# Graph attention on one core: TensorE takes the score banks of a tile in pairs, and the value matmuls sorted by width

## Chip, cores, metric

The kernel runs on one NeuronCore of a Trainium2 chip (trn2). The metric is the device time of one execution in microseconds, lower is better.

## The reference

Inputs are x (2048 x 256), adj (2048 x 2048, about 0.4% of its entries not zero) and four weight matrices, all float32. Eight heads; head h takes the rows 256h to 256h+255 of the flat projections, since `reshape(h, n, d)` splits rows and not columns.

```python
q = (x @ Wq).reshape(h, n, d)          # Wq, Wk, Wv: 256 x 2048
k = (x @ Wk).reshape(h, n, d)
v = (x @ Wv).reshape(h, n, d)
a = jnp.einsum('hnd,hmd->hnm', q, k) * scale + adj + adj
mask = adj == 0.0
a = jax.nn.softmax(jnp.where(mask, -1000000.0, a), axis=-1)
a = jnp.where(mask, 0.0, a)
out = jnp.einsum('hnm,hmd->hnd', a, v)
out = out.transpose(1, 0, 2).reshape(n, h * d) @ Wout
return layernorm(x + out)
```

## The kernel before, in words

All matrix products run in float32r, each operand split into a high and a low part, and a product is made of high x high, high x low and low x high. Wout is folded into v, so that a head's values are already the output's 256 columns.

**Tiles.** The work is 8 heads x 16 tiles of 128 query rows, numbered tau = 16 h + t. A tile has 2048 key columns, in 4 banks of 512. `scores(tau, b)` (L398 to L412) makes one bank with six matmuls of 512 columns (L409). `values(tau, g)` (L414 to L435) multiplies the probabilities of four blocks of 128 keys with v: for each block one matmul of 512 columns (high part of p with both parts of v, L428 and L432) and one of 256 columns (low part of p with the high part of v, L430), into `y_bank`. The two are issued in turn, 256 then 512.

**Projections.** The projections of a head are made between the scores, from one 256 x 256 weight slice each: `k` (eight, c = 0 to 7), `q` (eight), `vt` (eight, x times Wv, turned) and `v` (eight, from vt and Wout). Each is twelve matmuls of 256 columns (L374). `x` is turned once per head (L394). The function `due(tau, b)` (L175 to L193) and the tables `FIRST_V`, `LATER_V`, `FIRST_K` and `NEXT_K` (L166 to L173) say which ones follow the scores of bank b in tile t. Within a head after the first: tile 0: k7, q1; tile 1: vt0; tile 2: vt1, q2, v0 to v3 and vt2 to vt5; tile 3: v4 to v7, vt6, vt7; tiles 4, 6, 8, 10, 12: one q; tile 13: the turn of the next x; tile 14: q0 of the next head; tile 15: k0 to k6 of the next head, as (k0), (k1, k2), (k3, k4), (k5, k6) behind the four banks. Tiles 5, 7, 9, 11 have none.

**Order on TensorE** (L441 to L453): for each tile, for each bank: six score matmuls, the projections due, then the values of bank g of tile tau - 3 (`LAG`). So a quiet tile is four times (6 of 512, then 4 times 256 + 512). The first value matmul of a tile waits until all four pieces of p are split (`p_lo`).

**Banks and evictions.** Scores and projections rotate through a ring of six PSUM banks, in the order in which they are issued; `own(key)` waits until the one six places before is emptied. A projection is evicted by ScalarE (`hi_of`, L526) and then VectorE (`lo_of`, L613 or L617); a score bank by VectorE (L630), which adds the mask and keeps the maximum. After the fourth bank VectorE takes the row maximum (L642), ScalarE exp (L532), VectorE the 32 x 32 transpose (L653), and DMAs on SP (L306) and on ScalarE's queue (L569) shuffle it in four pieces. ScalarE then copies each piece to the high part (`hi_p`, L541) and GpSimd subtracts for the low part (`lo_p`, L480). `hi_p` of tile tau - 2 runs in the round of tile tau; its first piece waits for `y_done`, the end of the values of two tiles earlier.

**Weights.** A slice is loaded by SP (L267) into one of five slots as soon as the projection five places earlier is done. ScalarE converts it (`hi_w`, L518) and GpSimd subtracts (`lo_w`, L469), and `project_x` waits for `w_lo` (L380). Both look ahead by the same count: after ScalarE has evicted the projection of weight n it converts up to weight n + 2 (L593 to L595), and GpSimd follows in the same place of its queue (L502 to L504):

```python
for b in range(BANKS):
    if 2 <= tau < ALL + 2 and b < 2:
        hi_p(tau - 2, 2 * b)
        hi_p(tau - 2, 2 * b + 1)
    ...
    for key in due(tau, b):
        hi_of(key)
        if key in w_order:
            hi_w(w_order[key] + 3)
```

So ScalarE's, GpSimd's, VectorE's and SP's queues all follow `due`: two pieces of p stand ahead of the projections of bank 0, the other two between those of bank 0 and of bank 1. SP loads the weights up to bank i's last key plus five before it shuffles piece i of the tile before (L331 to L335).

In head 0 the masks are built from adj by VectorE, ScalarE and GpSimd and stored; from head 1 on ScalarE's queue loads 1 MB per tile (`load_m`, L552).

Of the kernel before, what the change touches and what calls it, by code (L numbers as in the profile page):

```python
# [29 lines left out]
def graph_attention_layernorm(nc, x, adj, wq, wk, wv, wout, out):  # L30
# [14 lines left out]
    with ExitStack() as ctx:  # L45
# [113 lines left out]
        def in_order(key):  # L159
            give_home(key)  # L160
            if key[0] in ("k", "q", "vt"):
# [7 lines left out]
        LATER_V = {(1, 3): (("vt", 0),), (2, 0): (("vt", 1),), (2, 1): (("v", 0), ("vt", 2), ("v", 1), ("vt", 3)),  # L169
                   (2, 2): (("v", 2), ("vt", 4)), (2, 3): (("v", 3), ("vt", 5)), (3, 0): (("v", 4), ("vt", 6)),  # L170
                   (3, 1): (("v", 5), ("vt", 7)), (3, 2): (("v", 6), ("v", 7))}
# [4 lines left out]


# [69 lines left out]
        with nc.Block() as block:  # L247
# [111 lines left out]
            def _(pe):  # L359
# [6 lines left out]
                def wait_emptied(key):  # L366
                    r, fill = home[key]
                    pe.wait_ge(emptied[r], fill)
# [45 lines left out]
                def values(tau, g):  # L414
                    h, t = divmod(tau, TILES)
                    y = y_bank[tau % 2]
                    if g == 0:
                        pe.wait_ge(p_lo, 4 * (tau + 1))
                        if tau >= 2:
                            pe.wait_ge(y_added, tau - 1)  # L420
                    if t == 0:
                        wait_emptied(("v", h, 2 * g))
                        wait_emptied(("v", h, 2 * g + 1))
                    for j in range(TPB * g, TPB * (g + 1)):
                        hi, lo = (p_split[tau % 2][:, part, j * P:(j + 1) * P] for part in (HI, LO))
                        first, last = j == 0, j == CHUNKS - 1
                        if first:
                            nc.tensor.matmul(y[:], hi, v_split[:, j].rearrange("p s d -> p (s d)"),  # L428
                                             start=True, stop=False)
                        nc.tensor.matmul(y[:, 0:D], lo, v_split[:, j, HI], start=False, stop=False)  # L430
                        if not first:
                            mm = nc.tensor.matmul(y[:], hi, v_split[:, j].rearrange("p s d -> p (s d)"),  # L432
                                                  start=False, stop=last)
                    if g == BANKS - 1:
                        mm.then_inc(y_done, 1)  # L435
# [5 lines left out]
                for tau in range(ALL + LAG):  # L441
                    for g in range(BANKS):
# [9 lines left out]
                        if tau >= LAG:  # L452
                            values(tau - LAG, g)  # L453
# [352 lines left out]
```

## Time and profile before

| | |
|---|---|
| median of 3 runs | 1853.81 us (1853.4 to 1855.88) |
| the profiled execution | 1851.97 us, span 1850.2 us |
| TensorE matmul | 1808.3 us busy (98%), 10272 matmuls |
| TensorE weight loads | 1580.0 us (85%), beside the matmuls |
| VectorE, GpSimd, ScalarE | 1117.0, 983.8, 851.5 us |
| granted TensorE clock | 0.995 of full, mean over the span |
| chain of waits that ended last | 87% TensorE |

The span is cut by the profiler from the first to the last instruction; the run's own time is 1.8 us longer. Matmuls overlap: the next one starts before the last has drained, so what a matmul costs is the distance of starts, not the mean duration in the table of groups. A row of the timeline merges instructions of one line ("x6"), and the number in brackets at its end is the idle time of the engine before it with what ended it.

### The profile page before, as it was taken

What the parts mean: (1) busy time and instruction counts of PE and PEld (TensorE: products, weight loads), DVE (VectorE), ACT (ScalarE), POOL (GpSimd) and SP (SyncE); (2) the same over time, 40 slices, a digit from 0 to 9 for tenths busy, and PEclk for the clock granted to TensorE, in tenths of its full rate; (3) what the DMA queues carried; (4) which work ended last, traced back from release to release, by engine and by line L of the source; (5) the groups of instructions that cost most, each with busy time, mean ns of one, the idle gap of its engine ahead of it and who ended that gap; (6) DMA issues with size and microseconds to landing.
All of it is one profiled execution on the core that took longest, in us unless ns stands there. A gap on an engine that the chain in (4) does not pass through costs nothing.

```text
span 1850.2 us, 29363 instructions
## 1 busy us (share of the span) xinstructions
PE 1808.3 (98%) x10272; PEld 1580.0 (85%) x10272; DVE 1117.0 (60%) x2316; ACT 851.5 (46%) x1411; POOL 983.8 (53%) x764
## 2 busy tenths in 40 slices
PE   7989899999999999999999999999999999999997
PEld 6978788888898888988889888888888888898886
DVE  6788855555555555555655555555555556556667
ACT  4645554344554444544454444544454444554442
POOL 6787765444644446444564445634455444544443
PEclk9999999999999999999999999999999999999999
DMA  7787765666656666566664666656665566655664
GB/s 229 226 283 238 249 211 156 177 191 186 195 147 187 191 195 182 150 185 186 199 187 143 194 185 190 181 157 194 189 187 168 160 197 196 189 166 155 180 180 116
DMA packets 186962, 345.96 MB, mean 187 GB/s; under 512 B 39360, under 2 KB 96704, under 8 KB 170432
## 3 DMA queue, kind: packets, MB, share of 16 engines
q1 hardware_dynamic: 146112, 193.06, 37.2%
q10 hardware_dynamic: 40704, 151.03, 25.5%
q8 instruction: 82, 1.34, 0.3%
q14 instruction: 64, 0.52, 0.1%
HBM read 190.84 MB, written 18.87 MB: 113 GB/s over the span
## 4 chain that ended last, share of the span: by engine, by line
PE 87%; DVE 3%; issue 1%; SPq 1%; DMA 0%; POOL 0%; ACT 0%; DVEq 0%; ACTq 0%
PE bank L409 34%; PE y_bank L432 22%; PE bank L374 17%; PE y_bank L430 12%; PE y_bank L428 1%; SPq L306 1%; DVE blocks L653 1%; DVE zero_mark L691 0%; DVE y_acc L743 0%; POOL p_split L480 0%; DVE t_p L630 0%; DVE m_sb L697 0%; DMA raw_x<-in_x_dram 0%; PE bank L394 0%; ACT m_sb L560 0%
## 5 line engine op out<-in xcount | busy, mean ns | idle before, releaser
L480 POOL TENSOR_TENSOR p_split<-p_turned,p_split 128x512 fp32r<-128x512 f32 x512 | 651.5, 1301 | 628.7 <-ACT p_split L541 628.1
L409 PE MATMUL bank<-k_split,q_split 128*128 128x512 f32 x3072 | 790.0, 392 | 0.0
L432 PE MATMUL y_bank<-v_split,p_split 128*128 128x512 f32 x1920 | 701.8, 399 | 0.0
L409 PEld LDWEIGHTS bank<-k_split,q_split 128*128 128x128 f32 x3072 | 577.4, 188 | 110.5 <-issue 0.3
L630 DVE CUSTOM_DVE_ANT_0 t_p<-bank,m_sb 128x512 f32<-128x512 f32 x512 | 351.2, 687 | 339.9 <-PE bank L409 317.5
L430 PE MATMUL y_bank<-v_split,p_split 128*128 128x256 f32 x2048 | 555.7, 282 | 0.0
L532 ACT ACTIVATE t_p<-t_p,small 128x2048 f32<-128x2048 f32 x128 | 256.8, 2006 | 442.3 <-DVE small L642 442.3
L432 PEld LDWEIGHTS y_bank<-v_split,p_split 128*128 128x128 f32 x1920 | 362.7, 189 | 76.1
L430 PEld LDWEIGHTS y_bank<-v_split,p_split 128*128 128x128 f32 x2048 | 389.1, 190 | 18.7
L541 ACT ACTIVATE p_split<-p_turned 128x512 fp32r<-128x512 f32 x512 | 291.9, 620 | 167.1 <-DMA p_turned<-blocks 166.9
L653 DVE STREAM_TRANSPOSE blocks<-t_p 128x2048 f32<-128x2048 f32 x128 | 295.9, 2312 | 106.3 <-ACT t_p L532 74.1
L469 POOL TENSOR_TENSOR w_slot<-raw_w,w_slot 128x512 fp32r<-128x512 f32 x192 | 250.1, 1305 | 199.5 <-ACT w_slot L518 197.4
L374 PE MATMUL bank<-x_t,w_slot 128*128 128x256 f32 x2304 | 305.2, 284 | 11.6 <-issue 9.7
L374 PEld LDWEIGHTS bank<-x_t,w_slot 128*128 128x128 f32 x2304 | 296.5, 192 | 23.0 <-issue 11.9
L518 ACT ACTIVATE w_slot<-raw_w 128x512 fp32r<-128x512 f32 x192 | 119.7, 623 | 12.6 <-DMA raw_w<-in_L_gnn_Wk_dram 9.8
L374 PEld LDWEIGHTS bank<-w_out,vt_split 128*128 128x128 f32 x768 | 98.7, 191 | 6.1 <-POOL w_out L474 2.8
L374 PE MATMUL bank<-w_out,vt_split 128*128 128x256 f32 x768 | 101.2, 283 | 2.4 <-POOL w_out L474 2.4
L675 DVE SCALAR_TENSOR_TENSOR y_acc<-y_bank,small,y_acc 128x256 f32<-128x256 f32 x128 | 61.9, 484 | 48.8 <-PE y_bank L432 48.5
L486 POOL TENSOR_TENSOR m_sb<-m_sb,blocks 128x512 f32<-128x512 f32 x46 | 76.8, 1682 | 21.0 <-ACT m_sb L560 20.5
L526 ACT ACTIVATE v_split<-bank 128x512 fp32r<-128x512 f32 x64 | 38.2, 596 | 91.1 <-PE bank L374 91.1
L526 ACT ACTIVATE vt_split<-bank 128x512 fp32r<-128x512 f32 x64 | 38.3, 598 | 88.6 <-PE bank L374 88.6
L613 DVE SCALAR_TENSOR_TENSOR q_split<-bank,q_split 128x512 fp32r<-128x512 f32 x64 | 44.2, 690 | 52.9 <-ACT q_split L526 52.9
(45 smaller groups left out, 716.3 us busy)
## 6 DMA issues: line engine op xcount, KB each, us to landing
m_sb<-m_dram ACTq DMA_DIRECT2D x112, 1024.0 KB, 5.4
p_turned<-blocks SPq DMA_DIRECT2D x1536, 64.0 KB, 2.2
p_turned<-blocks ACTq DMA_DIRECT2D x512, 64.0 KB, 2.3
raw_w<-in_L_gnn_Wk_dram SPq DMA_DIRECT2D x64, 256.0 KB, 3.8
blocks<-in_adj_dram SPq DMA_DIRECT2D x64, 256.0 KB, 4.4
raw_w<-in_L_gnn_Wq_dram SPq DMA_DIRECT2D x64, 256.0 KB, 3.7
m_dram<-m_sb SPq DMA_DIRECT2D x16, 1024.0 KB, 6.6
raw_w<-in_L_gnn_Wv_dram SPq DMA_DIRECT2D x64, 256.0 KB, 3.8
```

Source lines behind the costliest of these rows:

```text
L374: mm = nc.tensor.matmul(dst[:, o * R:(o + 1) * R], left[:, a, k, o * P:(o + 1) * P], right[:, b, k, :], start=(i == 0), stop=(i == len(TER ...
L409: mm = nc.tensor.matmul(dst[:], q[:, a, k, f * P:(f + 1) * P], k_split[:, kk, k, b * BANK:(b + 1) * BANK], start=(i == 0), stop=(i == len( ...
L430: nc.tensor.matmul(y[:, 0:D], lo, v_split[:, j, HI], start=False, stop=False)
L432: mm = nc.tensor.matmul(y[:], hi, v_split[:, j].rearrange("p s d -> p (s d)"), start=False, stop=last)
L469: nc.gpsimd.tensor_tensor(w[:, LO], raw_slot[n % SLOTS][:], w[:, HI].bitcast(F32), ALU.subtract).then_inc(w_lo, 1)
L480: nc.gpsimd.tensor_tensor(lo, p_turned[:, i * BANK:(i + 1) * BANK].rearrange("p (j b) -> p j b", b=QUAD), hi.bitcast(F32), ALU.subtract).t ...
L486: nc.gpsimd.tensor_tensor(m_piece(a), m_piece(a), adj_place[q].rearrange("p (r c) -> p c r", c=C), ALU.add).then_inc(m_by_pool, 1)
L518: nc.scalar.activation(w[:, HI], raw_slot[n % SLOTS][:], ACT.Copy).then_inc(w_hi, 1)
L532: nc.scalar.activation(t_p[:], t_p[:], ACT.Exp, bias=neg_max[:, t:t + 1], scale=1.0, accum_out=row_sum[:, t:t + 1]).then_inc(exp_done, 1)
L541: nc.scalar.activation(by_chunk(p_split[tau % 2][:, HI])[:, :, i, :], p_turned[:, i * BANK:(i + 1) * BANK].rearrange("p (j b) -> p j b", b ...
L630: nc.vector.tensor_tensor_reduce(out=t_p[:, b * BANK:(b + 1) * BANK], in0=bank[r][:], in1=m_sb[tau % 2][:, b * BANK:(b + 1) * BANK], scale ...
L653: nc.vector.transpose(turned_place(tau)[:].rearrange("p (q j b) -> p j q b", q=QUADS, b=QUAD), t_p[:].rearrange("p (j q b) -> p j q b", q= ...
```

## The change

TensorE takes two banks at a time: twelve score matmuls, the projections due in both banks, then the values of two banks, first eight matmuls of 512 columns and then eight of 256. `due` yields nothing at even banks and the keys of both banks at odd ones, on every engine. In a head after the first, v0 to v3 and v4 to v7 are moved so that a part of v is overwritten only after the values of the head before have read it: tile 2 makes v0 vt2 v1 vt3 v2 vt4 v3 vt5 behind bank 3, tile 3 makes v4 vt6 v5 vt7 v6 v7 behind bank 1. Tile 15 makes k0 k1 k2 behind bank 1 and k3 k4 k5 k6 behind bank 3. The number of matmuls and their operands are unchanged, and so are all waits, but for their place.

```diff
--- before.py
+++ after.py
@@ -166,14 +166,20 @@
         FIRST_V = {(0, 3): (("vt", 0), ("vt", 1)), (1, 0): (("v", 0), ("vt", 2)), (1, 1): (("v", 1), ("vt", 3)),
                    (1, 2): (("v", 2), ("vt", 4)), (1, 3): (("v", 3), ("vt", 5)), (2, 0): (("v", 4), ("vt", 6)),
                    (2, 1): (("v", 5), ("vt", 7)), (2, 2): (("v", 6),), (2, 3): (("v", 7),)}
-        LATER_V = {(1, 3): (("vt", 0),), (2, 0): (("vt", 1),), (2, 1): (("v", 0), ("vt", 2), ("v", 1), ("vt", 3)),
-                   (2, 2): (("v", 2), ("vt", 4)), (2, 3): (("v", 3), ("vt", 5)), (3, 0): (("v", 4), ("vt", 6)),
-                   (3, 1): (("v", 5), ("vt", 7)), (3, 2): (("v", 6), ("v", 7))}
+        LATER_V = {(1, 3): (("vt", 0),), (2, 0): (("vt", 1),), (2, 2): (("v", 0), ("vt", 2), ("v", 1), ("vt", 3)),
+                   (2, 3): (("v", 2), ("vt", 4), ("v", 3), ("vt", 5)), (3, 0): (("v", 4), ("vt", 6)),
+                   (3, 1): (("v", 5), ("vt", 7), ("v", 6), ("v", 7))}
         FIRST_K = {(0, 0): (4, 5), (0, 1): (6, 7)}
         NEXT_K = {(TILES - 1, 0): (0,), (TILES - 1, 1): (1, 2), (TILES - 1, 2): (3, 4), (TILES - 1, 3): (5, 6)}
 
         def due(tau, b):
 
+
+            if b % 2:
+                yield from due_by_bank(tau, b - 1)
+                yield from due_by_bank(tau, b)
+
+        def due_by_bank(tau, b):
 
             h, t = divmod(tau, TILES)
             if h >= H:
@@ -411,27 +417,24 @@
                                               start=(i == 0), stop=(i == len(TERMS) - 1))
                     mm.then_inc(scores_done, 1)
 
-                def values(tau, g):
+                def values(tau, pair):
                     h, t = divmod(tau, TILES)
                     y = y_bank[tau % 2]
-                    if g == 0:
+                    if pair == 0:
                         pe.wait_ge(p_lo, 4 * (tau + 1))
                         if tau >= 2:
                             pe.wait_ge(y_added, tau - 1)
                     if t == 0:
-                        wait_emptied(("v", h, 2 * g))
-                        wait_emptied(("v", h, 2 * g + 1))
-                    for j in range(TPB * g, TPB * (g + 1)):
-                        hi, lo = (p_split[tau % 2][:, part, j * P:(j + 1) * P] for part in (HI, LO))
-                        first, last = j == 0, j == CHUNKS - 1
-                        if first:
-                            nc.tensor.matmul(y[:], hi, v_split[:, j].rearrange("p s d -> p (s d)"),
-                                             start=True, stop=False)
-                        nc.tensor.matmul(y[:, 0:D], lo, v_split[:, j, HI], start=False, stop=False)
-                        if not first:
-                            mm = nc.tensor.matmul(y[:], hi, v_split[:, j].rearrange("p s d -> p (s d)"),
-                                                  start=False, stop=last)
-                    if g == BANKS - 1:
+                        for c in range(4 * pair, 4 * (pair + 1)):
+                            wait_emptied(("v", h, c))
+                    chunks = range(2 * TPB * pair, 2 * TPB * (pair + 1))
+                    for j in chunks:
+                        nc.tensor.matmul(y[:], p_split[tau % 2][:, HI, j * P:(j + 1) * P],
+                                         v_split[:, j].rearrange("p s d -> p (s d)"), start=(j == 0), stop=False)
+                    for j in chunks:
+                        mm = nc.tensor.matmul(y[:, 0:D], p_split[tau % 2][:, LO, j * P:(j + 1) * P],
+                                              v_split[:, j, HI], start=False, stop=(j == CHUNKS - 1))
+                    if pair == BANKS // 2 - 1:
                         mm.then_inc(y_done, 1)
 
                 pe.wait_ge(ident_ready, 1)
@@ -449,8 +452,8 @@
                                 project_v(key)
                             else:
                                 project_x(key)
-                        if tau >= LAG:
-                            values(tau - LAG, g)
+                        if tau >= LAG and g % 2:
+                            values(tau - LAG, g // 2)
 
             @block.gpsimd
             def _(pool):
```

## Rows read from the trace of the kernel before

**Rows 1.** The page, part 1: busy us (share of the span) xinstructions of each engine.

```profile
PE 1808.3 (98%) x10272; PEld 1580.0 (85%) x10272; DVE 1117.0 (60%) x2316; ACT 851.5 (46%) x1411; POOL 983.8 (53%) x764
```

**Rows 2.** Windows: stretch and length in us, busy (x), PEclk, DMA share, GB/s.

```profile
400.00:1800.00 1400.00, 1400.00 (x7979) 1.00 0.61 180
...
795.09:806.22 11.13, 11.13 (x58) 9.40 (x57) 6.43 (x14) 4.37 (x8) 5.07 (x4) 1.00 0.63 182
```

**Rows 3.** Timeline of TensorE in a tile without projections: start us, us, instruction.

```profile
797.88 1.52 PE L409 MATMUL bank<-k_split,q_split 128*128 128x512 f32 x6
799.24 0.28 PE L430 MATMUL y_bank<-v_split,p_split 128*128 128x256 f32 x1
...
800.64 1.54 PE L409 MATMUL bank<-k_split,q_split 128*128 128x512 f32 x6
802.02 0.28 PE L430 MATMUL y_bank<-v_split,p_split 128*128 128x256 f32 x1
```

**Rows 4.** Timeline of TensorE early in head 0, runs of one width.

```profile
44.23 1.55 PE L409 MATMUL bank<-k_split,q_split 128*128 128x512 f32 x6
45.62 1.60 PE L374 MATMUL bank<-w_out,vt_split 128*128 128x256 f32 x12
47.05 1.60 PE L374 MATMUL bank<-x_t,w_slot 128*128 128x256 f32 x12
48.49 1.55 PE L409 MATMUL bank<-k_split,q_split 128*128 128x512 f32 x6
```

**Rows 5.** Timeline of TensorE, tile 15 of head 3 and the next start.

```profile
913.99 1.54 PE L409 MATMUL bank<-k_split,q_split 128*128 128x512 f32 x6
...
919.59 3.04 PE L374 MATMUL bank<-x_t,w_slot 128*128 128x256 f32 x24
...
925.26 3.04 PE L374 MATMUL bank<-x_t,w_slot 128*128 128x256 f32 x24
928.13 0.28 PE L430 MATMUL y_bank<-v_split,p_split 128*128 128x256 f32 x1
...
935.21 0.62 PE L409 MATMUL bank<-k_split,q_split 128*128 128x512 f32 x2
```

**Rows 6.** Timeline of ScalarE and its DMA queue in the same tile.

```profile
913.82 0.33 ACTq L552 DMA_DIRECT2D m_sb<-m_dram  x1
...
916.00 1.14 ACT L541 ACTIVATE p_split<-p_turned 128x512 fp32r<-128x512 f32 x2
...
919.49 0.63 ACT L541 ACTIVATE p_split<-p_turned 128x512 fp32r<-128x512 f32 x1 [0.83 <-DMA p_turned<-blocks]
921.22 0.60 ACT L526 ACTIVATE k_split<-bank 128x512 fp32r<-128x512 f32 x1 [1.10 <-PE bank L374]
...
926.89 0.60 ACT L526 ACTIVATE k_split<-bank 128x512 fp32r<-128x512 f32 x1 [3.11 <-PE bank L374]
```

**Rows 7.** Timeline of GpSimd in the same tile.

```profile
919.21 1.31 POOL L469 TENSOR_TENSOR w_slot<-raw_w,w_slot 128x512 fp32r<-128x512 f32 x1
920.49 2.55 POOL L480 TENSOR_TENSOR p_split<-p_turned,p_split 128x512 fp32r<-128x512 f32 x2
...
928.09 2.72 POOL L469 TENSOR_TENSOR w_slot<-raw_w,w_slot 128x512 fp32r<-128x512 f32 x2 [2.54 <-ACT w_slot L518]
```

**Rows 8.** TensorE waits on weights, heads 0 and 1; windows at two waits of head 0.

```profile
243.90 1.72 PE L374 MATMUL bank<-x_t,w_slot 128*128 128x256 f32 x12 [3.65 <-issue]
...
299.31 1.67 PE L374 MATMUL bank<-x_t,w_slot 128*128 128x256 f32 x12 [1.18 <-issue]
...
187.00:192.00 5.00, 2.36 (x12) 1.00 0.94 335
...
245.00:250.00 5.00, 5.00 (x22) 0.66 0.36 111
```

**Rows 9.** Timeline of VectorE: the eviction behind ScalarE's at 921.22.

```profile
921.85 0.69 DVE L617 TENSOR_TENSOR k_split<-bank,k_split 128x512 fp32r<-128x512 f32 x1 [1.10 <-ACT k_split L526]
```

**Rows 10.** Timeline of ScalarE: the last exp.

```profile
1821.42 2.01 ACT L532 ACTIVATE t_p<-t_p,small 128x2048 f32<-128x2048 f32 x1 [6.76 <-DVE small L642]
```

## Prediction

> **What bounds the kernel now.** I read the engine totals first: TensorE is busy 1808.3 us of a span of 1850.2, and nothing else passes 1117 [rows 1]. The windows then say where the missing 42 us lie. From 400 to 1800 us TensorE is busy in all 1400 us at a granted clock of 1.00 [rows 2]; its idle time is outside: the start, the building of the masks in head 0, the first head switch, and the end. So from head 1 on the time is the length of TensorE's own queue: an edit pays only if it makes that queue shorter, and any new wait in it is paid in full.
>
> The queue's length has to be read from starts, since durations overlap. In the timeline of a quiet tile six score matmuls take 1.36 us from the first's start to the next group's (0.2267 each), the four pairs of value matmuls that follow 1.40, and six score matmuls right behind such pairs 1.38 [rows 3]. Where runs of one width follow each other, twelve 256-column matmuls take 1.43 to 1.44 (0.1196 each) and six 512-column ones behind them 1.38 to 1.39 [rows 4]. In alternation a 256 and a 512 cost 0.350; apart they cost 0.2267 + 0.1196 = 0.346, and every bank's scores pay for the return as well. Coming back from 256 to 512 costs some 0.026 once, over the next six matmuls.
>
> **Part 1, the value matmuls in runs.** A tile without projections takes 11.13 us [rows 2]. After: 40 of 512 x 0.2267 = 9.07, two returns x 0.026 = 0.05, 16 of 256 x 0.119 = 1.91 (the first of a run follows in 0.114), together 11.03: 0.10 less. A tile with projections keeps those runs as they are, but has one return more: 0.07 to 0.09 less. By the tables five tiles of a later head have none; the head gains 5 x 0.10 + 11 x 0.08 = 1.39 us. Seven heads: -9.7. Head 0 waits for data in half of its tiles; I take -0.5 of a possible -1.3. Term: **-10.2**.
>
> Eight 512-column value matmuls in a row don't occur in the trace. If alternation is not what costs, the term is 0; if the 256-column ones also ran at half the clean 512 (0.1133), it would be 2048 x 0.006 = 12 us more. I stay at the row of the same width. What speaks against the change is a rule of the Trainium skill, "TensorE: Matmul & The Clock Gate", Back-to-back issue gap: spacing is columns over 2.4 GHz plus 2.5 ns, whatever the neighbour, 215.8 and 109.2 ns. By it the order is worth nothing and the sum would be 10.2 higher. The rows give 226.7 and 119.6, and more in alternation, so here the rows disagree with it.
>
> **Part 2, bank 3's scores come earlier in the tile.** They now end 2.8 us before the tile's end, not 1.4, so maximum, exp and transpose start 1.4 earlier. In mid-kernel TensorE waits for none of them: 0. At the end it counts: the last exp starts at 1821.42 [rows 10], the split of tile 126 follows, and values(126) waits for it, values(127) behind it. That chain moves up 1.4: **-1.4**. In head 0 scores of bank 1 now stand ahead of the wait for p_lo, which shortens single waits by up to 1.4; but the x turn in tile 13 waits for its load and now has one more value group behind it. Together 0, bounds -5 and +4.
>
> **Part 3, projections of two banks stand in a row.** This is the dear part. A weight is prepared only two keys ahead: ScalarE converts w(n+2) after it has evicted projection n (L518 behind L526), GpSimd subtracts (L469), and TensorE waits for w_lo. From ScalarE's eviction start to GpSimd's end is 926.89 to 928.09 + 1.3 = 2.5 us [rows 6, 7]; with the step from the last matmul to ScalarE (the first projection begun at 919.59 ends its 1.44 at 921.03, ScalarE starts at 921.22: 0.19) 2.7 us. Today four value pairs and six scores (2.8) stand between two groups and cover it. In a row there is one projection between n and n+2: 1.44 [rows 4]. Two places of each head switch have three or more weights of one kind in a row.
>
> (a) Tile 15, second pair: k3 k4 k5 k6 stand in a row. Today k5 starts two blocks after k4 ends at 928.13; its weight is ready at 929.4 [rows 5, 7]. After: k5 waits 1.3, and the restart behind a wait costs 0.07 (twelve matmuls take 1.67 instead of 1.60 [rows 4, 8]). k6's weight is then ready in time. 1.35 x 7 = **+9.5**.
>
> (b) Tile 15, first pair: k0 k1 k2. TensorE reaches k2 at start + 2.77 + 2.88 = 5.65 us. Its weight is converted after k0's eviction, and in ScalarE's and GpSimd's queues all four pieces of the p split of tile 13 now stand ahead of it; today only two do (GpSimd runs L469 between two pairs of L480). GpSimd's four pieces take 2 x 2.55 = 5.1 [rows 7]. They start 0.7 after ScalarE's first, which waits for exp and y_done: today start + 2.0 (916.00 against 913.99 [rows 5, 6]), after the change some + 0.7. GpSimd: 1.4 + 5.1 + 1.3 = 7.8, so at least 2.2 of wait. But the fourth piece also waits for its shuffle, which lands behind the 1 MB mask load issued at 913.82: ScalarE takes it at 919.49, 5.7 after that issue [rows 6]. The mask load moves up 2.5, together with q's weight load and the shuffle itself. Landing at + 5 to + 6 gives k2's weight at 8.3 to 9.5 and a wait of 2.6 to 3.9. I take 3.0 for six heads: **+18**. Head 0's switch already waits 3.65 there today [rows 8]; two more pieces of 1.27 stand ahead: **+2.5**.
>
> (c) Tile 3: v7 follows vt7 with only v6 between, and needs vt7 evicted by ScalarE and VectorE: 0.19 + 0.63 + 0.69 [rows 6, 9] plus a wake-up is 1.6 against 1.44. 0.25 x 7 = **+1.8**. Tile 2's eight projections alternate v and vt, so weights stand 2.9 apart and vt two projections ahead of its v: 0.
>
> That two keys are too few is to be seen today: in tile 2 of head 1, where five projections stand in one bank and the p pieces came late, the fifth waited 1.18 us [rows 8].
>
> **Queues passed.** SP loads weights before it shuffles a piece. With all keys on odd banks pieces 0 and 2 no longer wait for projections, and 1 and 3 wait for the pair's last, which TensorE reaches a value group earlier than today: 0 for TensorE, as p_lo has time to spare (tile 13's is complete at 923.0 and its use begins after 935.2 [rows 5, 7]). ScalarE's own shuffles are no longer behind bank 2's eviction: earlier. The ring of six banks: after the eight projections each bank was filled 7 us before, evictions keep up; k7's eviction, now behind the p pieces, has 3 us left before bank 3 of the new head needs it. If that cover went, it would be 1 us per head.
>
> **Sum.** -10.2 - 1.4 + 9.5 + 18 + 2.5 + 1.8 = +20.2. The profiled execution took 1851.97 us (span 1850.2 and 1.8 around it): 1872.2. The median of the three runs shown is 1.8 higher than the profiled run, which would give 1874; I keep to the profiled one, as the runs' own spread is 2.5, and about 0.2% (3.7 us) is what can be told from no change. Forecast **1872**.
>
> **Rivals.**
> 1. *The clock falls too.* At head 0's switch TensorE was idle 3.65 us and the next window shows a clock of 0.66; at 187 to 192, with 2.36 of 5 us busy and so 2.64 idle, it stayed at 1.00 [rows 8]. A wait of 3.0 to 3.9 lies between. A window of 5 us at 0.66 costs 1.7; at six switches +10: 1882.
> 2. *The weights come in time* (faster than before): ScalarE or GpSimd runs further ahead than I schedule, so terms a to c are 0 and only -11.6 stays: 1840. It turns at a total wait of 1.7 us per switch: below that the change gains. For it: both engines are idle about half the time [rows 1]. Against: k2's and k5's conversions are behind an eviction in a fixed queue, and two waits of this kind are in the trace.
> 3. *The order of widths is free* (the rule above). Nothing is gained in the values, the waits stay: 1852 + 31.8 - 1.4 = 1882. Against: the alternation's extra is there in the rows [rows 3, 4] and in every quiet tile.
> 4. *The waits are at their lower ends* (k2 2.2, k5 1.2, v7 0, head 0 +0.5, and head 0 gains 3): 13.2 + 8.4 + 0.5 - 11.6 - 3 = +7.5: 1859.5.
>
> **Chances.** Forecast 0.52 (1864 to 1879), rival 1 0.17, rival 2 0.13, rival 3 0.04, rival 4 0.11, and 0.03 for waits of such a size that they cancel the gain. Faster 0.13, same 0.03, slower 0.84. The range reaches from rival 4's lower side to above rival 1: 1852 to 1888; it leaves out rival 2. Within the likeliest case it is 1864 to 1879.
>
> **What would show it.** Tiles without projections at 11.03 instead of 11.13 (part 1). New rows "PE L374 <- POOL w_slot L469" or "<- issue", two per head near the start and the second half of tile 15, of about 3.0 and 1.3 (a, b); a small L374 wait on VectorE's vt_split in tile 3 (c). TensorE's busy time in mid-kernel below 100%. The last exp 1.4 nearer to the end of the scores. If the L374 waits are missing, or add to less than 12 us, the forecast is wrong; if the granted clock shows 0.5 stretches at each switch, rival 1 holds.

## The result and the profile after

The changed kernel takes 1889.87 us (median of 6 runs, 1886.65 to 1895.1) where the kernel before takes 1856.34 in the same series: ratio 1.0183, 95% interval 1.0167 to 1.0199, some 34 us slower. The profiled executions are 1890.11 and 1851.97 us, 38.1 apart. Forecast were 1872 and a range up to 1888: the direction is right, the size is not.

The page of the changed kernel, its first part (against [rows 1]; its span is 1888.3 us):

```profile
PE 1817.1 (96%) x10272; PEld 1596.7 (85%) x10272; DVE 1160.5 (61%) x2316; ACT 853.1 (45%) x1411; POOL 983.3 (52%) x764
```

TensorE has 9 us more of busy time for the same 10272 matmuls, and idles 29 us more. Its waits between 400 and 1830 us (us in total, times, longest); before there was none on a weight there:

```profile
PE bank L380 <- issue: 21.0, 12, 3.4
```

These are twelve waits at the six switches from head 1 to head 7. The starts of the tiles in both timelines of TensorE tell where the 38.1 us lie: up to the start of head 1 +14.2 (273.89 against 259.68), in head 1 +2.7, in heads 2 to 6 +23.5, in head 7 and the end -2.4.

**A quiet tile**, head 3 tile 5 (against [rows 2, 3]; L415 scores, L432 the 512-column value matmuls, L435 the 256-column ones, start and us first):

```profile
815.96 2.91 PE L415 MATMUL bank<-k_split,q_split 128*128 128x512 f32 x12
818.70 1.98 PE L432 MATMUL y_bank<-v_split,p_split 128*128 128x512 f32 x8
820.52 1.11 PE L435 MATMUL y_bank<-v_split,p_split 128*128 128x256 f32 x8
...
826.98 1.32 PE L415 MATMUL bank<-k_split,q_split 128*128 128x512 f32 x5
```

From 815.96 to 826.98 are 11.02 us; before it was 11.13 [rows 2]. Twelve scores and eight values of 512 columns take 4.56 together (0.228 each with the return), eight of 256 take 0.95 (0.119 each), as the runs of one width did before [rows 4].

**Tile 15 of head 3** (against [rows 5]; L380 are the projections), up to the start of head 4:

```profile
934.00 2.91 PE L415 MATMUL bank<-k_split,q_split 128*128 128x512 f32 x12
936.74 3.03 PE L380 MATMUL bank<-x_t,w_slot 128*128 128x256 f32 x24
941.83 2.20 PE L380 MATMUL bank<-x_t,w_slot 128*128 128x256 f32 x12 [2.06 <-issue]
943.83 3.07 PE L432 MATMUL y_bank<-v_split,p_split 128*128 128x512 f32 x8
...
947.68 2.91 PE L415 MATMUL bank<-k_split,q_split 128*128 128x512 f32 x12
950.42 3.03 PE L380 MATMUL bank<-x_t,w_slot 128*128 128x256 f32 x24
954.62 3.13 PE L380 MATMUL bank<-x_t,w_slot 128*128 128x256 f32 x24 [1.16 <-issue]
...
960.38 0.86 PE L415 MATMUL bank<-k_split,q_split 128*128 128x512 f32 x3
```

26.4 us instead of 21.2. k0 and k1 are the 24 matmuls at 936.74; k2 starts only at 941.83. In the second pair k5 starts at 954.62, behind 1.16 us of idleness. And one thing more: the eight value matmuls at 943.83 take 3.07 us where the same eight take 2.00 at 957.58 and 1.98 in the quiet tile. They are slow, not late.

The timeline of GpSimd in that tile (against [rows 7]; L483 pieces of p, L472 weights):

```profile
935.29 5.21 POOL L483 TENSOR_TENSOR p_split<-p_turned,p_split 128x512 fp32r<-128x512 f32 x4 [1.40 <-ACT p_split L544]
940.46 2.50 POOL L472 TENSOR_TENSOR w_slot<-raw_w,w_slot 128x512 fp32r<-128x512 f32 x2
...
953.25 1.27 POOL L472 TENSOR_TENSOR w_slot<-raw_w,w_slot 128x512 fp32r<-128x512 f32 x1 [6.71 <-ACT w_slot L521]
```

The timeline of ScalarE and its DMA queue (against [rows 6]; L555 mask load, L544 pieces of p, L529 eviction, L521 weight):

```profile
931.42 0.39 ACTq L555 DMA_DIRECT2D m_sb<-m_dram  x1
...
934.59 1.67 ACT L544 ACTIVATE p_split<-p_turned 128x512 fp32r<-128x512 f32 x3
938.51 0.63 ACT L544 ACTIVATE p_split<-p_turned 128x512 fp32r<-128x512 f32 x1 [2.26 <-DMA p_turned<-blocks]
939.05 0.58 ACT L529 ACTIVATE k_split<-bank 128x512 fp32r<-128x512 f32 x1
939.53 0.62 ACT L521 ACTIVATE w_slot<-raw_w 128x512 fp32r<-128x512 f32 x1
```

GpSimd subtracts four pieces of p (5.21 us from 935.29) before it comes to k2's weight at 940.46; TensorE could have used that weight at 939.6. The shuffle of the fourth piece, which I had feared behind the mask load of 931.42, came only just in time: ScalarE took that piece at 938.51 and ended its copy at 939.14, GpSimd was through with the third at 939.11 and began the fourth at 939.23. Heads 1, 2, 3, 4 and 6 are alike in this, within 0.4 us. In head 5 the shuffle was late, and the wait for k2 is the longest of the six. ScalarE's fourth piece there, and TensorE's k2:

```profile
1397.52 0.63 ACT L544 ACTIVATE p_split<-p_turned 128x512 fp32r<-128x512 f32 x1 [3.59 <-DMA p_turned<-blocks]
```

```profile
1400.82 2.90 PE L380 MATMUL bank<-x_t,w_slot 128*128 128x256 f32 x12 [3.37 <-issue]
```

For k5 the weight's turn on GpSimd comes at 953.25, behind the eviction of k3.

**The clock.** Windows of TensorE in this tile (stretch, length, busy, PEclk, DMA share, GB/s):

```profile
935.00:940.00 5.00, 4.78 (x33) 1.00 0.53 169
940.00:945.00 5.00, 3.17 (x15) 0.77 0.40 115
945.00:950.00 5.00, 5.00 (x25) 0.89 0.70 186
```

and at the switches of head 1 and head 5:

```profile
480.00:485.00 5.00, 3.82 (x29) 1.00 0.49 146
485.00:490.00 5.00, 4.02 (x26) 1.00 0.54 157
1398.00:1403.00 5.00, 2.18 (x10) 0.71 0.36 113
```

At the ends of heads 2 to 6 the granted clock fell to its lower level (1.2 of 2.4 GHz) about where the wait for k2 ends, in head 5 for twice as long. In head 1 it stayed at 1.00, though the wait for k2 was 2.15 us there and 2.01 to 2.28 in heads 2, 3, 4 and 6. Tile 15 took 24.93 us in head 1, and 26.33, 26.38, 26.61, 28.91 and 26.52 in heads 2 to 6. With the idle time of its two waits taken off, that is 1.54 to 1.56 us more than in head 1 for heads 2, 3, 4 and 6, and 2.76 for head 5.

**Head 0.** Waits of TensorE there, the longest among them:

```profile
20.15 2.10 PE L415 MATMUL bank<-k_split,q_split 128*128 128x512 f32 x6 [2.44 <-DVE k_split L620]
...
72.71 2.90 PE L380 MATMUL bank<-x_t,w_slot 128*128 128x256 f32 x12 [3.83 <-issue]
...
209.85 1.66 PE L415 MATMUL bank<-k_split,q_split 128*128 128x512 f32 x6 [1.91 <-DVE small L633]
218.61 1.09 PE L400 MATMUL bank<-ident,raw_x 128*128 128x128 f32 x4 [7.11 <-DMA raw_x<-in_x_dram]
...
254.27 2.90 PE L380 MATMUL bank<-x_t,w_slot 128*128 128x256 f32 x12 [5.57 <-issue]
```

20.15: scores of bank 1 now follow bank 0's at once and need k3 evicted. 72.71: tile 2 makes v4 vt6 q2 v5 vt7 in a row, three weights of one stretch. 209.85 waits for VectorE to empty a bank, 218.61 for the load of the next x: 7.1 us, where it was 4.3. 254.27 is k2 at head 0's switch.

### The profile page after: what moved, and what is told of

It is laid out like the page before. It is cut to its first block, busy times and chain, and to the rows that moved or that the text cites. A ratio compares the mean times of both kernels' runs of the same rounds, so it can differ in the third digit from the quotient of the medians.

```text
span 1888.3 us, 29363 instructions
## 1 busy us (share of the span) xinstructions
PE 1817.1 (96%) x10272; PEld 1596.7 (85%) x10272; DVE 1160.5 (61%) x2316; ACT 853.1 (45%) x1411; POOL 983.3 (52%) x764
## 3 DMA queue, kind: packets, MB, share of 16 engines
q8 instruction: 82, 1.34, 0.3%
## 4 chain that ended last, share of the span: by engine, by line
PE 85%; SPq 3%; DVE 2%; issue 2%; DMA 1%; POOL 0%; ACT 0%; ACTq 0%; DVEq 0%
PE bank L415 33%; PE y_bank L432 22%; PE bank L380 17%; PE y_bank L435 11%; SPq L312 2%; DMA p_turned<-blocks 1%; DVE blocks L656 1%; DVE y_acc L746 0%; POOL p_split L483 0%; DVE zero_mark L694 0%; DMA raw_x<-in_x_dram 0%; PE bank L400 0%; DVE t_p L633 0%; ACTq L572 0%; ACT m_sb L563 0%
## 5 line engine op out<-in xcount | busy, mean ns | idle before, releaser
L483 POOL TENSOR_TENSOR p_split<-p_turned,p_split 128x512 fp32r<-128x512 f32 x512 | 651.0, 1298 | 618.8 <-ACT p_split L544 617.4
L415 PE MATMUL bank<-k_split,q_split 128*128 128x512 f32 x3072 | 746.9, 392 | 6.5 <-DVE k_split L620 4.0
L415 PEld LDWEIGHTS bank<-k_split,q_split 128*128 128x128 f32 x3072 | 560.5, 189 | 114.0 <-issue 5.3
L432 PE MATMUL y_bank<-v_split,p_split 128*128 128x512 f32 x2048 | 519.3, 396 | 4.0 <-POOL p_split L483 4.0
L432 PEld LDWEIGHTS y_bank<-v_split,p_split 128*128 128x128 f32 x2048 | 384.8, 192 | 80.9 <-POOL p_split L483 4.8
L544 ACT ACTIVATE p_split<-p_turned 128x512 fp32r<-128x512 f32 x512 | 292.6, 621 | 253.4 <-DMA p_turned<-blocks 253.2
L472 POOL TENSOR_TENSOR w_slot<-raw_w,w_slot 128x512 fp32r<-128x512 f32 x192 | 247.9, 1296 | 246.8 <-ACT w_slot L521 246.5
L380 PE MATMUL bank<-x_t,w_slot 128*128 128x256 f32 x2304 | 312.3, 290 | 41.4 <-issue 35.3
L380 PEld LDWEIGHTS bank<-x_t,w_slot 128*128 128x128 f32 x2304 | 301.6, 197 | 52.6 <-issue 43.9
L435 PEld LDWEIGHTS y_bank<-v_split,p_split 128*128 128x128 f32 x2048 | 279.6, 190 | 20.3
L435 PE MATMUL y_bank<-v_split,p_split 128*128 128x256 f32 x2048 | 285.6, 282 | 0.0
L521 ACT ACTIVATE w_slot<-raw_w 128x512 fp32r<-128x512 f32 x192 | 119.7, 624 | 12.2 <-DMA raw_w<-in_L_gnn_Wk_dram 10.7
L380 PE MATMUL bank<-w_out,vt_split 128*128 128x256 f32 x768 | 103.6, 285 | 2.2 <-POOL w_out L477 2.0
L663 DVE SCALAR_TENSOR_TENSOR small<-small 128x1 f32<-128x1 f32 x128 | 103.3, 807 | 0.0
L380 PEld LDWEIGHTS bank<-w_out,vt_split 128*128 128x128 f32 x768 | 98.2, 193 | 5.1 <-POOL w_out L477 2.4
L620 DVE TENSOR_TENSOR k_split<-bank,k_split 128x512 fp32r<-128x512 f32 x64 | 44.0, 690 | 64.6 <-ACT k_split L529 64.4
L529 ACT ACTIVATE k_split<-bank 128x512 fp32r<-128x512 f32 x64 | 37.9, 592 | 89.9 <-PE bank L380 89.8
```

The source lines that it names most:

```text
L380: mm = nc.tensor.matmul(dst[:, o * R:(o + 1) * R], left[:, a, k, o * P:(o + 1) * P], right[:, b, k, :], start=(i == 0), stop=(i == len(TER ...
L415: mm = nc.tensor.matmul(dst[:], q[:, a, k, f * P:(f + 1) * P], k_split[:, kk, k, b * BANK:(b + 1) * BANK], start=(i == 0), stop=(i == len( ...
L432: nc.tensor.matmul(y[:], p_split[tau % 2][:, HI, j * P:(j + 1) * P], v_split[:, j].rearrange("p s d -> p (s d)"), start=(j == 0), stop=False)
L435: mm = nc.tensor.matmul(y[:, 0:D], p_split[tau % 2][:, LO, j * P:(j + 1) * P], v_split[:, j, HI], start=False, stop=(j == CHUNKS - 1))
L472: nc.gpsimd.tensor_tensor(w[:, LO], raw_slot[n % SLOTS][:], w[:, HI].bitcast(F32), ALU.subtract).then_inc(w_lo, 1)
L483: nc.gpsimd.tensor_tensor(lo, p_turned[:, i * BANK:(i + 1) * BANK].rearrange("p (j b) -> p j b", b=QUAD), hi.bitcast(F32), ALU.subtract).t ...
```

## The experiments

The theory after this reading (W): the weights' look-ahead of two keys covers the distance of banks, not projections in a row; its waits carry most of the loss, and the clock falls because of them. Beside it (H): in head 0 the projections in a row meet the building of the masks. Rivals: the waits come from the pieces of p or the loads, pairing as such costs, the sorting costs, or the clock falls without the waits.

**1. Look-ahead three** (label look3).

```diff
-                                lo_w(w_order[key] + 3)
+                                lo_w(w_order[key] + 4)
-                                hi_w(w_order[key] + 3)
+                                hi_w(w_order[key] + 4)
```

> The changed kernel with one edit: ScalarE and GpSimd prepare weights three keys ahead instead of two. Theory W (the waits on weights in tile 15 carry the loss, and the clock falls because of them): both waits of each switch go (k2's weight is then made behind q0 of the tile before, k5's behind k2), 7 x (2.3 + 1.4) = 26 us, and with them the half-clock stretches of heads 1 to 6, about 9 us; 1852 to 1858 in all, tile 15 of heads 1 to 6 at 21.1 us. What stays above the kernel before is head 0. Rival S (the waits come from the p pieces or the shuffles standing ahead in ScalarE's queue, whatever the look-ahead): k2's wait stays, 1875 or more. Rival C (the clock falls from the longer runs of 256-column matmuls, not from the waits): waits go but the granted clock still shows one 0.5 stretch per switch, about 1863.

Measured: 0.9987 (0.9978 to 0.9997), median 1851.41. The timeline of TensorE, starts of tile 15 of head 3 and of head 4:

```profile
921.81 2.91 PE L415 MATMUL bank<-k_split,q_split 128*128 128x512 f32 x12
...
942.95 1.32 PE L415 MATMUL bank<-k_split,q_split 128*128 128x512 f32 x5
```

Tile 15 takes 21.14 us in all of heads 1 to 6, no wait of TensorE is left from 300 to 1830 us, and no half-clock stretch between 262 and 1839. The two characters edited give back 36 us. Theory W holds; rivals S and C fall. Head 1 starts at 271.8 us, so most of head 0's loss stays, and the heads behind it take 223.5 us instead of 224.6.

**2. Only the sorting** (sort_only), on the kernel before:

```diff
-                    for j in range(TPB * g, TPB * (g + 1)):
...
+                    chunks = range(TPB * g, TPB * (g + 1))
+                    for j in chunks:
+                        nc.tensor.matmul(y[:], p_split[tau % 2][:, HI, j * P:(j + 1) * P],
+                                         v_split[:, j].rearrange("p s d -> p (s d)"), start=(j == 0), stop=False)
+                    for j in chunks:
+                        mm = nc.tensor.matmul(y[:, 0:D], p_split[tau % 2][:, LO, j * P:(j + 1) * P],
+                                              v_split[:, j, HI], start=False, stop=(j == CHUNKS - 1))
```

> The kernel before with one part of the change: the eight value matmuls of a bank as four of 512 and then four of 256 columns; banks one by one, projections where they were. Theory W: a bank is 10 x 0.2267 + 0.026 + 0.47 = 2.77 us instead of 2.79, a quiet tile 11.06 to 11.07 instead of 11.13, 128 tiles: 7 to 8 us less, 1844 to 1846, no new wait. Rival (the order of widths is free): 11.13 and 1852. Rival (sorting itself brings the loss, as p_lo or v are needed in another order): above 1856 with waits at L428.

Measured: 0.9979 (0.9969 to 0.9988), median 1850.02. A quiet tile, from the start of its scores to the next tile's:

```profile
793.82 1.55 PE L409 MATMUL bank<-k_split,q_split 128*128 128x512 f32 x6
...
804.89 1.32 PE L409 MATMUL bank<-k_split,q_split 128*128 128x512 f32 x5
```

11.07 us, as worked out. The gain in time (4 us by the ratio, and between the profiled executions) is less than the 7 to 8 expected, which took 0.06 for all 128 tiles: a quiet tile gains that, the others in heads 2 to 6 mostly 0.03 to 0.05, so a head takes 223.95 us for 224.59. Head 0 is 0.9 shorter up to head 1's start, and head 1 takes 0.5 longer.

**3. Projections with their own bank** (keys_by_bank), else as changed:

```diff
-            if b % 2:
-                yield from due_by_bank(tau, b - 1)
-                yield from due_by_bank(tau, b)
+            yield from due_by_bank(tau, b)
```

> The changed kernel with one part undone: the projections stay with their own bank on every engine (scores 0, its projections, scores 1, its projections, then the values of both banks); the value matmuls and the tables for v as in the change. Theory W: k0 and k1, and k4 and k5, have six score matmuls (1.38) between them, which with one projection makes 2.8 us against the 2.7 that a weight needs; at most 0.1 to 0.3 of wait per place, quiet tiles at 11.03; head 0 near the kernel before: 1841 to 1847, clock at 1.00 after head 0. Rival (pairing the banks on TensorE is what costs, not where the projections stand): 1870 or more.

Measured: 0.9971 (0.9960 to 0.9982), median 1848.65. Tile 15 of head 3 and head 4's start:

```profile
914.66 1.55 PE L413 MATMUL bank<-k_split,q_split 128*128 128x512 f32 x6
...
935.93 1.32 PE L413 MATMUL bank<-k_split,q_split 128*128 128x512 f32 x5
```

21.27 us: 0.12 above look-ahead three, with two more returns from 256 to 512 columns in it, so six score matmuls between k0 and k1 all but cover the weight. Pairing on TensorE is not what costs; where the projections stand is. Head 1 starts at 264.1 us, 4.4 later than before, which is why the time lies above the 1841 to 1847 expected.

**4. Head 0 in the old order** (head0_old): `due` by bank and values by bank for tau < 16.

```diff
-            if b % 2:
+            if tau < TILES:
+                yield from due_by_bank(tau, b)
+            elif b % 2:
...
-                        if tau >= LAG and g % 2:
+                        if LAG <= tau < TILES:
+                            values_by_bank(tau - LAG, g)
+                        elif tau >= LAG and g % 2:
```

> The changed kernel, with head 0 (its 16 tiles) in the order of the kernel before on all engines and heads 1 to 7 as changed. Theory W plus H (head 0 loses 14 us by itself, as its projections in a row meet the building of the masks on VectorE and the late load of the next x): first tile of head 1 starts near 260 us instead of 273.9, the rest as in the change, 1876 in all. Rival (head 0's loss is made up later, or is a consequence of the same weight waits): no better than 1885.

Measured: 1.0141 (1.0124 to 1.0158), median 1879.25; head 1 starts at 262.0 us. The waits of heads 1 to 6 are nearly the same, 12 times, 21.0 us. Head 0 is worth 8 us by the ratios and 12 by the starts of head 1. The clock fell at the switches of heads 2 to 5; at those of heads 1 and 6 it stayed at 1.00 behind waits of 2.12 and 2.21 us, and tile 15 took 24.89 and 24.99 us.

**5. k2 moved behind bank 3** (k2_moved), look-ahead two:

```diff
-        NEXT_K = {(TILES - 1, 0): (0,), (TILES - 1, 1): (1, 2), (TILES - 1, 2): (3, 4), (TILES - 1, 3): (5, 6)}
+        NEXT_K = {(TILES - 1, 0): (0,), (TILES - 1, 1): (1,), (TILES - 1, 2): (2, 3, 4), (TILES - 1, 3): (5, 6)}
```

> The changed kernel (look-ahead two) with one key moved: tile 15 makes k0 k1 behind bank 1 and k2 k3 k4 k5 k6 behind bank 3, so the first of the two waits has no place and five keys stand in a row. Theory W: no wait in the first half of tile 15; in the row, k4's weight is made behind k2's eviction and waits 1.3, k6's is then nearly in time: 1.4 to 1.6 in all, tile 15 at 22.5 to 22.8 us in heads 1 to 6 instead of 24.9 to 28.9. Theory K (the clock falls because of the 2.2 us wait): no half-clock stretch in heads 1 to 6, 1862 to 1868 in all. Rival (the fall comes from the sum of the waits of a tile or from any wait over 1 us): a stretch per head remains, tile 15 at 24.2 or more, 1873.

Measured: 1.0086 (1.0072 to 1.0099), median 1871.14. Tile 15 of head 3 in the timeline of TensorE:

```profile
924.37 2.91 PE L415 MATMUL bank<-k_split,q_split 128*128 128x512 f32 x12
...
939.72 3.12 PE L380 MATMUL bank<-x_t,w_slot 128*128 128x256 f32 x24 [1.16 <-issue]
943.99 1.66 PE L380 MATMUL bank<-x_t,w_slot 128*128 128x256 f32 x12 [1.15 <-issue]
...
948.28 1.09 PE L415 MATMUL bank<-k_split,q_split 128*128 128x512 f32 x4
```

The wait of the first pair is gone. In the row of five both k4 and k6 wait, 1.16 and 1.15; I had k6 nearly in time, which is wrong: each second key pays the whole difference. Tile 15 takes 23.91 us in each of heads 1 to 6, and none of them shows a half-clock stretch. So waits of 1.2 us don't bring the clock down here, and the falls of the changed kernel belong to the wait of 2.0 or more. The time is 18 us below the changed kernel's by the ratios and 22 in the profiles: 16 in the tiles 15 of heads 1 to 6 and 6.5 in head 0. It is above the 1862 to 1868 expected, by the wait for k6 among others.

**6. Look-ahead one on the kernel before** (look1_before): both `+ 3` become `+ 2`.

> The kernel before with its look-ahead cut from two keys to one: the suspected cost doubled, with the old order of banks and values. Theory W: each second weight of a bank waits the whole 2.7 us (k2, k4, k6), and in tile 2, where q2 v0 vt2 v1 vt3 stand in one bank, vt2 and vt3 wait 1.3 each: tile 15 at 21.2 + 8.1 = 29.3 us or more (with clock falls up to 34), tile 2 at 28.2, quiet tiles at 11.13 as before: 10.7 us per head plus the clock, 1930 to 1960 in all. Rival (the look-ahead is not what paces the weights; the pieces of p or the loads are): less than 4 us per head, under 1885.

Measured: 1.0741 (1.0722 to 1.0761), 1992 us. Two of the waits of tile 15 in head 3:

```profile
994.46 1.66 PE L374 MATMUL bank<-x_t,w_slot 128*128 128x256 f32 x12 [2.59 <-issue]
...
1003.00 2.63 PE L374 MATMUL bank<-x_t,w_slot 128*128 128x256 f32 x12 [2.59 <-issue]
```

Each second weight of a bank waits 2.59 us, for 2.7 worked out. From 300 to 1830 us there are 48 waits of 75.0 us together. The quiet tiles stay at 11.13. Tile 15 takes 33.7 to 35.3 us, tile 2 29.3 (30.2 in head 1): the clock is low for two or three stretches of 3.4 us at a switch and other weights wait too (0.85 at k1), and head 1 starts only at 289.3 us, so the total is above the 1930 to 1960 of the expectation. The look-ahead paces the old order as well; two keys were just enough for it.

**7. x turned later** (xturn_late), on look-ahead three:

```diff
-                if (t, b) == (TURN_X, 1):
+                if (t, b) == (TURN_X, 2):
```

> The kernel with look-ahead three, and x turned behind bank 3 of tile 13 instead of behind bank 1. Theory H: in head 0 TensorE waits for the load of the next x (7.1 us in the changed kernel, 4.3 in the one before), and with one value group and two score banks moved ahead of that wait tile 13 falls from 22.7 to 17 to 18 us; 1846 to 1848 in all, later heads unchanged. Rival (tile 13 is paced by the masks and by the p pieces, and the x wait only shows it): tile 13 or 14 takes it back, 1851.

Measured: 0.9984 (0.9975 to 0.9993), median 1851.41, the same time as look-ahead three and what the rival had. The timeline of TensorE in head 0, the x turn and a projection of tile 15:

```profile
218.21 0.63 PE L400 MATMUL bank<-ident,raw_x 128*128 128x128 f32 x4 [0.43 <-DMA raw_x<-in_x_dram]
...
246.24 2.35 PE L380 MATMUL bank<-x_t,w_slot 128*128 128x256 f32 x12 [4.35 <-POOL w_slot L472]
```

The wait for x fell to 0.43 us and tile 13 to 16.4. Tile 15 took it back: 33.6 us instead of 27.7, with a wait of 4.35 for a weight. In this profile head 1 still starts 3.3 us earlier, but the medians are alike. Head 0 is paced by more than one chain, and taking away one wait there shows the next.

**8. A version meant to be best** (best): head 0 sorted within banks, the rest changed, look-ahead three everywhere. The edit is that of experiment 4, with the value matmuls sorted within a bank as in experiment 2, and that of experiment 1.

> Head 0 bank by bank as in the kernel before, but its value matmuls sorted by width within a bank; heads 1 to 7 as in the change; look-ahead three everywhere. Theory W plus H: head 1 starts at 258 to 261 us as in the kernel before, each later head takes 223.5 us instead of 224.6, the end 1.4 less: 1851.97 - 0.9 - 7.6 - 1.4 = 1842 to 1844. Rival (head 0's start depends on the look-ahead too, or differs from run to run by more than is gained): 1847 to 1850.

Measured: 0.9977 (0.9967 to 0.9987), median 1850.46: the expectation was missed by 6 us, and the time is that of the rival. The later heads were at 223.5; but tile 1 of head 0 took 24.1 us instead of 19.7, with 4.5 us of waiting for Wout's split, and the first tile of head 1 18.8 instead of 14.2.

**9. The same with a late start** (best2): bank by bank and look-ahead two up to the first tile of head 1, from there paired and three.

```diff
+        PAIRED = TILES + 1
...
-            if tau < TILES:
+            if tau < PAIRED:
...
-                                lo_w(w_order[key] + 4)
+                                lo_w(w_order[key] + (4 if tau >= PAIRED else 3))
...
-                                hi_w(w_order[key] + 4)
+                                hi_w(w_order[key] + (4 if tau >= PAIRED else 3))
```

> Head 0 and the first tile of head 1 bank by bank with the look-ahead of two (so that the first weights and Wout are converted as in the kernel before), value matmuls sorted by width within a bank; from the second tile of head 1 on as in the change, with look-ahead three. Theory W plus H: head 1 starts at 257 to 261 us and its first tile takes 14 to 15 us (18.8 in the version that looked ahead three from the start), later heads 223.5 each: 1843 to 1847. Rival (the first 280 us vary by themselves by as much as separates the versions): no better than the 1848.7 of the kernel with the keys by bank.

Measured: 0.9951 (0.9938 to 0.9965), median 1844.88, as expected: faster than both kernels, 9 us (0.5%) below the one before. Head 1 starts at 260.7, its first tile takes 14.35, each of heads 2 to 6 takes 223.5 instead of 224.6.

**10. Both kernels once more** (before_again, after_again).

> The kernel before once more, for the scatter of head 0 between executions, with a profile. If head 0 scatters by several us, head 1 starts away from 259.7 (255 to 264) and the heads after it take 224.6 each again; if not, 259 to 260.5.

One execution of 1855.8 us. Head 1 starts at 261.9 us, heads 2 to 6 take 224.6 again.

> The changed kernel once more, with a profile. Waits in tile 15 of heads 1 to 6 the same to 0.1 us (2.2 and 1.3, they come from fixed durations); the half-clock stretches at some of the six switches, not at the same ones or in the same number: 4 to 7 stretches of 3.4 us; head 1 starts at 268 to 276 us.

One execution of 1889.41 us. Head 1 starts at 272.7; the waits of tile 15 are again 12 in number, 20.8 us, the one for k2 in head 5 again the longest (3.20); half-clock stretches again at the switches of heads 2 to 6, double in head 5, and not in head 1. Not only the number but the heads were the same, which I had not expected. Head 0 scatters by some 2 us between executions; the difference of the two kernels there is 14.2 in one pair and 10.7 in the other.

## Why the forecast was wrong

- **Part 1, values in runs** (-10.2): right. Quiet tiles are at 11.02 to 11.03, tiles with one projection at 12.49 for 12.57, and sorting within a bank gives 11.07. With the waits gone (look3) heads 2 to 6 take 1.10 us less than before, 1.34 without what v7 costs, for 1.39 worked out (a later head has four tiles without projections and one with only the turn of x, not five without). Rival 3 falls: the order of widths is worth what the rows said.
  The Trainium skill's formula in "TensorE: Matmul & The Clock Gate", Back-to-back issue gap, has only the matmul's own width in it (215.8 ns for 512 columns), and the page calls it the gap of isolated matmuls. It does not hold for these pairs of weight load and matmul, which start 226.7 ns apart.
- **Part 2, the end** (-1.4): the chain that I had named gave only about -0.3. The last exp starts 9.49 us after its tile's start instead of 10.95, so it did move up 1.46. But the values of tile 127 did not. First the timeline of TensorE, changed kernel, where the values of tiles 126 and 127 begin; then that of ScalarE with the last exp and the last piece of p; then that of VectorE between them:

```profile
1867.31 2.11 PE L432 MATMUL y_bank<-v_split,p_split 128*128 128x512 f32 x8 [0.68 <-POOL p_split L483]
...
1876.17 2.11 PE L432 MATMUL y_bank<-v_split,p_split 128*128 128x512 f32 x8 [3.01 <-POOL p_split L483]
```

```profile
1859.34 2.01 ACT L535 ACTIVATE t_p<-t_p,small 128x2048 f32<-128x2048 f32 x1 [6.64 <-DVE small L645]
...
1874.10 0.63 ACT L544 ACTIVATE p_split<-p_turned 128x512 fp32r<-128x512 f32 x1 [1.26 <-DMA p_turned<-blocks]
```

```profile
1861.15 0.48 DVE L678 SCALAR_TENSOR_TENSOR y_acc<-y_bank,small,y_acc 128x256 f32<-128x256 f32 x1 [1.85 <-PE y_bank L435]
...
1862.86 2.31 DVE L656 STREAM_TRANSPOSE blocks<-t_p 128x2048 f32<-128x2048 f32 x1
```

The first wait (tile 126) fell from 2.03 to 0.68, the second grew from 1.91 to 3.01. Between exp and shuffle stands VectorE: in its queue the eviction of the values of tile 124 comes before the transpose of tile 127, and it waits 1.85 us for TensorE to end them. So the transpose starts 13.00 us after the tile's start instead of 13.17, the shuffles behind it move up as little, and ScalarE stands 1.2 us for the last piece's shuffle. I had not followed the chain through VectorE's queue. From the start of tile 127 to the end of the program it is still 1.3 us less in this pair of profiles, 1.0 of it behind the last matmul, where I had forecast nothing; that the sum comes near 1.4 is luck. In the second pair it is 0.15.
- **Part 3 (a), k5** (1.35 per switch): right, 1.16 of idleness and, with the restart, 1.4 by the starts.
- **Part 3 (b), k2** (3.0): the mechanism and its schedule were right: GpSimd ends k2's weight 7.7 us after the tile's start, 7.8 was worked out. In five heads the size was that of the lower bound, 2.06 of idleness and 2.3 by the starts in head 3, as the fourth piece came just in time; in head 5 it came late and the wait was 3.37, inside the 2.6 to 3.9 that I had worked out for that case. Both waits together cost 3.78 per switch where I had 4.35, read from head 1's tile 15 (24.93), which has them without a clock fall; head 5 paid 1.2 more.
- **Part 3 (c), v7** (0.25): right, tile 3 takes 19.93 us for 19.78, against 0.09 less for the sorting: 0.24.
- **The clock** (rival 1, 0.17): the first step that failed. I took k2's wait as too short to bring the clock down, from one window with 2.64 us of idleness that stayed at 1.00. The sum had nothing for it. Here waits of 2.0 to 2.3 us, and the one of 3.37, brought it down in five of six heads. The tiles 15 of heads 2 to 6 take 28.65 us more than before, of which 5 x 3.71 is what head 1 shows without a fall. Of the 10.1 left, 1.1 are the longer wait of head 5, and **9.0 us** are the clock's: 1.54 to 1.56 in four heads and 2.76 in head 5. Experiments 1 and 5 show that it goes with the wait. Why it spared head 1 is open.
- **Head 0** ("Together 0, bounds -5 and +4", and +3.3 from the other parts): the second step that failed, +14.2 and +10.7 in the two pairs of profiles. In the first pair it loses 8.5 up to the end of tile 2, of which 5.3 in tile 2 with its five keys (6.8 in the second pair), where I had put waits for weights at 0 because I had gone through the table of the later heads only. Look-ahead three sets tile 2 to 15.56, as before. Tile 13 with the x wait takes 5.5 more and tile 15 with its weights 5.6 (k2 waits 5.57 there, where a weight waited 3.65 before), tiles 3 to 12 give 5.3 back. Of the x wait I had said that one more value group stands behind it, and priced that at nothing.
- The sum: 20.2 + 9.0 for the clock + 10.9 for head 0 - 3.4 for six switches of 3.78 + 1.1 for the late piece of head 5 + 0.1 at the end = 37.9, against 38.1 measured.
- Rival 2 (weights in time) is what experiments 1 and 9 make of the kernel: it was the mechanism in another kernel, not here. With look-ahead three the changed kernel gains, but less than 11.6, as head 0 keeps most of its loss.

What stays open: why head 5's shuffle came late, why head 1 kept its clock, and which of head 0's chains paces it once the weights are in time. Experiments 7 and 8 show only that a gain in one of its tiles is lost in a later one.

## What to carry to other kernels

Before work on a saturated engine is grouped, ask of every producer that follows the same list how many entries it runs ahead, and compare the time of that many entries in a row with the time it takes to make one. In the profiled pair the grouping was worth 11 us and what it brought on (waits, clock, head 0) cost 49. One more entry of look-ahead had room in the slots and cost nothing in the later heads; at the start it is not free, as experiments 8 and 9 show. And price a short wait of TensorE with the clock: here waits of 2.0 to 2.3 us cost 1.5 us more at most of the places.

## What the runs showed that I had not expected

- The length of a wait alone does not tell whether the clock falls. Waits of 2.0 to 2.3 us brought it down in heads 2 to 4 and 6 and not in head 1, in two executions of the changed kernel alike; in head0_old head 6 was spared too (2.21 us). Waits of 1.2 us never did in heads 1 to 6 of k2_moved (12 of them). In the kernel before, the clock fell behind 3.65 us of waiting at head 0's switch [rows 8]; in sort_only TensorE waited 3.25 us at the same place, and it stayed at 1.00. The windows of sort_only:

```profile
240.00:245.00 5.00, 1.75 (x15) 1.00 0.95 372
...
245.00:250.00 5.00, 5.00 (x35) 1.00 0.43 138
```

- The profile of look-ahead three gives a granted clock of 0.95 in the stretches where the others have 1.00, with tiles of the same length to 0.01 us; the window of a quiet tile of head 3:

```profile
803.77:814.79 11.02, 11.02 (x58) 0.95 0.60 173
```

A granted clock some per cent below 1.00 can thus stand in the records without the matmuls being slower.
- Six 512-column matmuls behind 256-column ones take 1.387 us, for scores and for values alike (1.387 to 1.395 in sort_only), and the seventh and later ones 0.2267 each.
